# A recommendation tower's interaction layer: tiles of 16 rows by 8 columns of d in place of 4 by 32, and one sum over d for each group of four tiles

## The reference

```python
x0 = inputs; prev = inputs; outs = []
for W in filters:                                  # [1024, 128], then [32*128, 128]
    z = jnp.einsum('bhd,bmd->bhmd', x0, prev)      # products of two fields at the same d
    b, h, m, d = z.shape
    z = z.reshape(b, h * m, d)
    cur = jax.nn.relu(jnp.einsum('bpd,pn->bnd', z, W[0]))
    prev = cur
    outs.append(cur)
return jnp.sum(jnp.concatenate(outs, axis=1), axis=-1)   # the sum over d
...
h = jnp.concatenate([z, dense_ctx], axis=1)
h = jnp.maximum(h @ W_top1 + b_top1, 0.0)
h = jnp.maximum(h @ W_top2 + b_top2, 0.0)
y = h @ W_top3
```

## Time and profile before

| | us |
|---|---|
| median of 3 runs | 900.58 (899.3 to 905.62) |
| the profiled execution | 904.71 |
| its span, first to last instruction | 902.9 |
| PE busy | 879.3 (97%) |
| ACT busy | 782.9 (87%) |
| DVE busy | 780.5 (86%) |
| POOL busy | 750.6 (83%) |

### The profile page before, as it was taken

One profiled execution on the slowest core, in us unless ns is written; L12 is line 12 of the kernel. 1 busy time (PEld: TensorE's weight loads), 2 busy tenths in 40 slices (PEclk: granted clock), 3 DMA queues, 4 the chain that ended last, 5 costly groups with the idle time before them and its releaser, 6 DMA issues.

```text
span 902.9 us, 17442 instructions
## 1 busy us (share of the span) xinstructions
PE 879.3 (97%) x3758; PEld 689.7 (76%) x3758; DVE 780.5 (86%) x903; ACT 782.9 (87%) x2744; POOL 750.6 (83%) x542
## 2 busy tenths in 40 slices
PE   3899999999999999999999999999999999999988
PEld 2678877777887777788777778877777887777844
DVE  4588888999888899988889998888989888898991
ACT  2699899999989999999989999989999999999942
POOL 5599889898888989888898988889899898988430
PEclk9999999999999999999999999999999999999987
DMA  5432222221222222122222212222221122220000
GB/s 179 127 115 79 80 74 78 78 64 34 67 78 73 77 78 68 33 64 78 73 77 78 68 35 61 78 73 77 78 75 33 56 78 73 77 78 1 1 1 0
DMA packets 42810, 60.85 MB, mean 67 GB/s; under 512 B 6274, under 2 KB 17154, under 8 KB 42787
## 3 DMA queue, kind: packets, MB, share of 16 engines
q1 hardware_dynamic: 38690, 58.48, 21.1%
q0 software_dynamic: 4096, 2.11, 1.6%
HBM read 56.37 MB, written 4.20 MB: 67 GB/s over the span
## 4 chain that ended last, share of the span: by engine, by line
PE 95%; DMA 1%; ACT 1%; DVE 1%; issue 1%; POOL 0%; SPq 0%; DVEq 0%; ACTq 0%; POOLq 0%
PE ps_y L637 27%; PE ps_y L643 26%; PE ps_y L638 26%; PE ps_c L616 6%; PE ps_h L648 2%; PE ps_c L625 2%; PE ps_c L624 2%; PE ps_c L626 2%; PE ps_c L622 1%; ACT prod L399 1%; PE ps_y L694 1%; PE ps_y L693 1%; DMA second<-et_scratch 1%; DMA gat<-table,rows_now 0%; POOL gat L292 0%
## 5 line engine op out<-in xcount | busy, mean ns | idle before, releaser
L399 ACT ACTIVATE prod<-ps_y,es 128x128 f32<-128x128 f32 x2560 | 715.7, 434 | 72.7 <-PE ps_y L643 68.7
L537 DVE TENSOR_REDUCE csum<-prod 128x64 f32<-128x1536 f32 x256 | 447.3, 1748 | 10.4
L637 PE MATMUL ps_y<-w_hi,c_hi 128*128 128x512 f32 x1024 | 437.3, 427 | 2.1 <-ACT prod L399 1.3
L643 PE MATMUL ps_y<-w_hi,c_lo 128*128 128x512 f32 x1024 | 400.9, 392 | 0.0
L638 PE MATMUL ps_y<-w_lo,c_hi 128*128 128x512 f32 x1024 | 400.4, 391 | 0.0
L330 POOL TENSOR_TENSOR prod<-prod 128x1024 f32<-128x1024 f32 x128 | 308.3, 2408 | 55.6 <-ACT prod L399 48.8
L523 DVE TENSOR_TENSOR prod<-ps_y,es 128x512 f32<-128x512 f32 x384 | 256.8, 682 | 76.2 <-PE ps_y L643 72.8
L637 PEld LDWEIGHTS ps_y<-w_hi,c_hi 128*128 128x128 f32 x1024 | 192.8, 188 | 54.7 <-issue 18.2
L638 PEld LDWEIGHTS ps_y<-w_lo,c_hi 128*128 128x128 f32 x1024 | 192.9, 188 | 50.2 <-issue 14.9
L643 PEld LDWEIGHTS ps_y<-w_hi,c_lo 128*128 128x128 f32 x1024 | 192.1, 188 | 43.4
L321 POOL TENSOR_TENSOR z<-first,second 128x512 f32<-128x512 f32 x155 | 198.6, 1299 | 9.1 <-DMA second<-et_scratch 9.1
(11 more groups left out here) (65 smaller groups left out, 278.0 us busy)
## 6 DMA issues: line engine op xcount, KB each, us to landing
second<-et_scratch SPq DMA_DIRECT2D x160, 256.0 KB, 4.4
first<-et_scratch SPq DMA_DIRECT2D x32, 256.0 KB, 3.3
et_scratch<-gat SPq DMA_DIRECT2D x64, 64.0 KB
prod<-w SPq DMA_DIRECT2D x4, 512.0 KB, 7.1
gat<-table,rows_now POOLq DMA_INDIRECT x128, 2.4
wt_sb<-wt SPq DMA_DIRECT2D x2, 512.0 KB
prod<-w0a SPq DMA_DIRECT2D x1, 320.0 KB, 3.0
prod<-w0b SPq DMA_DIRECT2D x1, 320.0 KB, 3.3
```

The source lines that it names most:

```text
L399: last = nc.scalar.activation(prod[:, buffer_of(g, u), h // 2, :, h % 2], ps_y[:, bank_of(g, u, k), j * N:(j + 1) * N], ACT.Copy, scale=es ...
L537: nc.vector.tensor_reduce(csum[:, maps, 0], prod[:, buffer_of(g, u), FOLD // 2:F // 2, maps, :].rearrange("p a n t -> p n a t"), AX.XY, AL ...
L637: nc.tensor.matmul(out, hi, w_hi, start=True, stop=False)
L643: nc.tensor.matmul(out, lo, w_hi, start=False, stop=True).then_inc(y_ready, 1)
```

## The change

A tile is now all 16 rows of its group by 8 of the 32 d: tile o holds d from 8o to 8o + 7. Nothing is summed over d until all four tiles of a group are there: their rectified results are added element by element, and one matmul against a `ones_b` of 128 x 16 sums the rest. In pieces:

- The rows of a group are dealt to the gathers in another order (`ids`, made before launch), `turn` reads `gat` in runs of 8 elements, the layer-0 matmuls read z in runs of 8 in place of 32, and `sum_h0` reads `c` in runs of 8. Number and size of instructions stay.
- `reduce` writes `csum[:, g.r, maps, u]`, a column for each tile.
- `rectify` (DVE, 128 times) and the zeroed column go. `rectify_parts` (ACT, once a group, at (1, 6) of the next group) rectifies all four columns, 512 elements; `add_parts` (DVE, once a group, at (2, 4)) adds them to 128.
- `sum_h1` runs once a group at (3, 3), with 16 columns.
- After the loop ACT runs `rectify_parts` of the last group, then DVE `add_parts`, and PE one `sum_h1`.
- `ones_b` comes by one more transfer on SP's queue (8 KB), ahead of the loads of w1, in place of the memsets.

```diff
-        csum = sb("csum", [P, N, 2])
-        c1 = sb("c1", [P, 2, N])
-        ones_b = sb("ones_b", [P, BT])
+        csum = sb("csum", [P, SLOTS, N, TG])
+        c1_parts = sb("c1_parts", [P, N, TG])
+        c1 = sb("c1", [P, SLOTS, N])
+        ones_b = sb("ones_b", [P, GB])
...
+            sp.dma_start(ones_b[:, :], ones_of_b).then_inc(ones_in, 16)
...
+            def rectify_parts(g):
+
+                act.wait_ge(reduced, g.times(TG * HALVES, TG * HALVES))
+                wait(act, c1_ready, g.times(1))
+                nc.scalar.activation(c1_parts[:, :, :], csum[:, g.r, :, :], ACT.Relu).then_inc(parts_rectified, 1)
+
...
+                        if (u, k) == (1, 6) and number != 0:
+                            rectify_parts(g.plus(-1))
...
+            rectify_parts(LAST)
+            for groups in (range(GROUPS - 1), range(GROUPS - 1, GROUPS)):
+                act.wait_ge(h1_done, groups.stop)
...
-                nc.vector.transpose(es[:, g.r, :, :].rearrange("p u f -> p (u f)"), gat[:, g.r, :]).then_inc(es_ready, 1)
+                nc.vector.transpose(es[:, g.r, :, :], gat[:, g.r, :].rearrange("p (u o d) -> p o u d", u=TG, d=DT)).then_inc(es_ready, 1)
...
-                    h0[:, bass.ds(g.times(TG * BT), TG * BT)], c[:, :].rearrange("p (t d) -> p t d", d=D),
-                    AX.X, ALU.add).then_inc(h0_done, 1)
+                    h0[:, bass.ds(g.times(GB), GB)], c[:, :].rearrange("p (o b d) -> p b o d", b=GB, d=DT),
+                    AX.XY, ALU.add).then_inc(h0_done, 1)
...
-            def rectify(g, u):
-
-                dve.wait_ge(reduced, g.times(TG * HALVES, (u + 1) * HALVES))
-                wait(dve, h1_done, g.times(TG, u - 1))
-                nc.vector.tensor_reduce(c1[:, u % 2, :], csum[:, :, :], AX.X, ALU.max).then_inc(c1_ready, 1)
+            def add_parts(g):
+
+                dve.wait_ge(parts_rectified, g.times(1, 1))
+                nc.vector.tensor_reduce(c1[:, g.r, :], c1_parts[:, :, :], AX.X, ALU.add).then_inc(c1_ready, 1)
...
-                    nc.tensor.matmul(ps_c[:, :], w0_sum[:, k, :], z[:, k, :].rearrange("p (b u d) -> p u b d", u=TG, b=BT),
+                    nc.tensor.matmul(ps_c[:, :], w0_sum[:, k, :], z[:, k, :].rearrange("p (b o d) -> p o b d", b=GB, d=DT),
                                      start=(k == 0), stop=False)
...
-            def sum_h1(g, u):
-
-                pe.wait_ge(c1_ready, g.times(TG, u + 1))
-                nc.tensor.matmul(ps_h1[:, bass.ds(g.times(TG * BT, u * BT), BT)], c1[:, u % 2, :], ones_b[:, :],
+            def sum_h1(g):
+
+                pe.wait_ge(c1_ready, g.times(1, 1))
+                nc.tensor.matmul(ps_h1[:, bass.ds(g.times(GB), GB)], c1[:, g.r, :], ones_b[:, :],
                                  start=True, stop=True).then_inc(h1_done, 1)
...
-                        if k == 3 and not (number == 0 and u < 3):
-                            sum_h1(*before(g, u, 3))
+                        if (u, k) == (3, 3) and number != 0:
+                            sum_h1(g.plus(-1))
```

More of the change, by code:

```diff
@@ L34 @@
 BT = P // D
+GB = 16
+DT = P // GB
 TILES = B // BT
@@ L103, with tower @@
 LAST = Group((GROUPS - 1) // SLOTS, (GROUPS - 1) % SLOTS)
-def tower(nc, ids, bounds, copy_of, table, dense_t, w0a, w0b, w1, wt1, bt1, wt2, bt2, wt3, y):
+def tower(nc, ids, bounds, copy_of, ones_of_b, table, dense_t, w0a, w0b, w1, wt1, bt1, wt2, bt2, wt3, y):
     ctx = ExitStack()
@@ L176, in tower @@
         w0_step = sem("w0_step")
-        ones_zeroed = sem("ones_zeroed")
-        csum_zeroed = sem("csum_zeroed")
+        ones_in = sem("ones_in")
         rows_staged = sem("rows_staged")
@@ L201, in tower @@
         reduced = sem("reduced")
+        parts_rectified = sem("parts_rectified")
         c1_ready = sem("c1_ready")
@@ L433, in _ @@
             over_groups(act, body)
-            for tiles in (range(TILES - 2), range(TILES - 2, TILES)):
-                act.wait_ge(h1_done, tiles.stop)
-                cols = slice(BT * tiles.start, BT * tiles.stop)
+            rectify_parts(LAST)
+            for groups in (range(GROUPS - 1), range(GROUPS - 1, GROUPS)):
+                act.wait_ge(h1_done, groups.stop)
+                cols = slice(GB * groups.start, GB * groups.stop)
                 nc.scalar.activation(h1_hi[:, cols], ps_h1[:, cols], ACT.Copy).then_inc(h1_hi_ready, 1)
@@ L463, in _ @@
             nc.vector.tensor_scalar(rows[:, :], neg[:, :], bounds_sb[:, 2:3], None, ALU.add).then_inc(rows_step, 1)
[L465 to L470, removed]
             dve.wait_ge(w0_in, 48)
@@ L534, in reduce @@
                     dve.wait_ge(dve_scaled, signals(DVE_BANKS, g, u, NK - 1))
-                    wait(dve, c1_ready, g.times(TG, u))
                 maps = slice(half * N // HALVES, (half + 1) * N // HALVES)
-                nc.vector.tensor_reduce(csum[:, maps, 0], prod[:, buffer_of(g, u), FOLD // 2:F // 2, maps, :].rearrange("p a n t -> p n a t"),
+                nc.vector.tensor_reduce(csum[:, g.r, maps, u], prod[:, buffer_of(g, u), FOLD // 2:F // 2, maps, :].rearrange("p a n t -> p n a t"),
                                         AX.XY, ALU.add).then_inc(reduced, 1)
-            def rectify(g, u):
-                dve.wait_ge(reduced, g.times(TG * HALVES, (u + 1) * HALVES))
-                wait(dve, h1_done, g.times(TG, u - 1))
-                nc.vector.tensor_reduce(c1[:, u % 2, :], csum[:, :, :], AX.X, ALU.max).then_inc(c1_ready, 1)
+            def add_parts(g):
+                dve.wait_ge(parts_rectified, g.times(1, 1))
+                nc.vector.tensor_reduce(c1[:, g.r, :], c1_parts[:, :, :], AX.X, ALU.add).then_inc(c1_ready, 1)
             for k in range(NK):
@@ L579, in body @@
                             reduce(*before(g, u, 2), 1)
-                        if k == 4 and not (number == 0 and u < 2):
-                            rectify(*before(g, u, 2))
+                        if (u, k) == (2, 4) and number != 0:
+                            add_parts(g.plus(-1))
                         if k == 6 and not (number == 0 and u == 0):
@@ L596, in _ @@
             reduce(LAST, TG - 2, 1)
-            rectify(LAST, TG - 2)
             for half in range(HALVES):
                 reduce(LAST, TG - 1, half)
-            rectify(LAST, TG - 1)
+            add_parts(LAST)
             dve.wait_ge(h1_hi_ready, 2)
@@ L619, in layer0 @@
                 pe.wait_ge(z_lo_ready, g.times(SPLIT, k + 1 - WHOLE))
-                high, low = (x[:, k, :].rearrange("p (b u d) -> p u b d", u=TG, b=BT) for x in (z_hi, z_lo))
+                high, low = (x[:, k, :].rearrange("p (b o d) -> p o b d", b=GB, d=DT) for x in (z_hi, z_lo))
                 if k == LASTK:
@@ L677, in body @@
                             layer0(g.plus(1), z_used_at.index((u, k)))
-                        if k == 3 and not (number == 0 and u < 3):
-                            sum_h1(*before(g, u, 3))
+                        if (u, k) == (3, 3) and number != 0:
+                            sum_h1(g.plus(-1))
             over_groups(pe, body)
-            sum_h1(LAST, TG - 3)
             pe.wait_ge(top_in, 7 * 16)
@@ L695, in _ @@
             pe.wait_ge(h1_hi_ready, 1)
-            sum_h1(LAST, TG - 2)
-            sum_h1(LAST, TG - 1)
+            sum_h1(LAST)
             pe.wait_ge(top_lo_ready, 2)
@@ L767 @@
     arrays = {
-        "ids": np.ascontiguousarray(x["ids"].reshape(TILES, BT, F).transpose(1, 2, 0).reshape(P, TILES)),
+        "ids": np.ascontiguousarray(x["ids"].reshape(GROUPS, BT, TG, F).transpose(1, 3, 0, 2).reshape(P, TILES)),
         "bounds": np.tile(np.stack([counts - 1, counts, bases], 1).astype(np.float32), (BT, 1)),
         "copy_of": np.tile(np.array([[0, 0], [1, 0], [0, -1], [0, 0]], np.float32), (F, 1)),
+        "ones_of_b": np.kron(np.eye(GB, dtype=np.float32), np.ones((DT, 1), np.float32)),
         "table": np.concatenate(tables),
```

2 lines of the change are left out of this document (1 added, 1 removed).

## The result

| | before | after |
|---|---|---|
| median of 4 runs each, us | 899.94 (898.35 to 905.62) | 873.47 (872.53 to 874.27) |
| the profiled execution, us | 904.71 | 874.27 |
| its span, us | 902.9 | 872.5 |
| mean granted clock over the span, of 2.4 GHz | 0.989 | 0.996 |

The ratio of the times is 0.969, with a 95% interval of 0.966 to 0.973: 26.5 us faster, where 877 with a range of 871 to 889 was forecast. Seven more runs of the changed kernel in a later comparison gave 873.87 beside 898.09.

A forecast was written before the change was run, and what follows sets the result against it. PE's own instruction sequence was taken to bound the loop, DVE holding PE up in the last group. Terms of -20.9 + 0.6 - 2.6 - 0.5 = -23.4 us took the median 900.6 to 877, range 871 to 889.

The forecast's parts named there:

- Term 1: PE's sums over d: 91 fewer at 0.23 us, -20.9 us; 16 columns in the 30 that stay, +0.6 us.
- Term 2: Layer-0 matmuls on PE reading z in runs of 8: taken as 0, up to +9.1 us, a gain excluded.
- Two thirds to all of the excess: Layer-0 matmuls: this share of their 0.013 us over plain ones is there without breaks, as in the top network.
- Term 3: New ACTIVATE on ACT behind bank (1, 6): at most 0.8 us a group, hidden from PE, cost 0.
- 0.6 are left: ACT's waits of 2.1 us a group, less 0.8 new work and 0.7 shorter group, leave 0.6 us.
- Rival 4: ACT's new work delays PE's ring in each group: 19 to 25 us come back, 896 to 902; chance 0.08.
- Term 4: Work leaving DVE: worth nothing in the loop; in the last group L693 starts 2.6 us earlier.
- Term 5: The end: 16 fp32 instructions keep 14.0 us at the low clock; the last two sums become one, -0.5 us.
- other case: At the end the clock stays at 2.4 GHz: fp32 instructions take 7 us, PE waits for DVE, 4.6 us sooner.
- The start: Before the loop: the memsets lie beside transfers, one more 8 KB transfer goes ahead of w1's; cost 0.

The follow-up runs named there:

- The experiment: The changed kernel with the last group's two casts of the top weights moved from DVE to ACT: 870.85 us, ratio 0.966 to the kernel before.

## Why the prediction was right

**Term 1** held: 0.233 us a sum by experiment, 0.23 in the prediction; 30 groups x 0.700 = 21.0 us. The 16 columns, put at +0.6, cost nothing that a start shows (0.915 us for the three steps with a sum before and after; the trace before held no sum of 16, so that only the profile after bears this out). The Trainium skill's floor of about 25 ns (TensorE: Matmul & The Clock Gate, section Back-to-back issue gap), taken as the whole cost, would by estimate have made three sums 0.15 us; the chip took 0.70. The two instructions of a sum do start 0.026 us apart; the cost stands behind them, 0.112 to the next plain matmul and another 0.085 to the one after. That exposed weight loads are the reason, as the prediction says, was not tested.

**Term 2** was put at 0, with a gain ruled out, and there was one. "A gain is excluded: nothing is read in longer runs than before" took for granted that longer runs can't be worse. Runs of 8 gave 0.087 us a group against runs of 32 128 elements apart, 30 x 0.087 = 2.6 us. Start by start, the kernel with three sums put back differs from the kernel before only from chunk 2's first matmul on. The two triples, each with the three plain matmuls behind it, are 0.026 and 0.025 us shorter. Much of the rest is in layer-1 matmuls further behind: the nine that follow chunk 2's start 0.227 us apart on average where it had been 0.229 (0.021 us in all), and the stretch up to chunk 4 gives another 0.017. In the kernel before with chunk 2 read in runs of 8, chunk 2 and what follows up to chunk 3 got shorter by the same 0.047 us. So how layer 0 reads z is the cause, and it also works on the matmuls behind, most of which lie outside the table's six steps. ("Two thirds to all of the excess" for contiguous operands was misread, too: 0.70 between 0.68 and 0.72 is half by the earlier trace rows.) The table's rows follow neither the length of the runs nor their distance in a simple way, and why they differ by some nanoseconds stays open. With terms 1 and 2 the loop's 23.6 us are accounted for.

**Term 3** came to the right conclusion by wrong numbers. ACT got 0.52 us a group, not 0.8, since its records overlap; and it had at least 3.0 us of room, not the 2.1 of its waits. "0.6 are left" was at least 1.7. Rival 4 was therefore further off than its 0.08: between two and six more such instructions, not at the first.

**Term 4** foresaw 2.6 us in the last group and got 1.7. The missing 0.9 is, as far as 0.8 of it goes, the cast that became longer beside the fold. The prediction had taken durations in the last group as fixed. PE's ring waits at (2, 2) for DVE's bank (1, 4), which stands directly behind this cast: the bank ends at 835.40 and PE goes on at 835.55, after a wait of 1.17 us (858.56, 858.71 and 0.69 before). The experiment shows that DVE paces this stretch; that the 0.8 comes from the place of the fold rests on the two pairs of timelines and on the DVE rectifier, where moving it was tried.

**Term 5** took the low clock as before. The profile shows its "other case", and its price: 4.6 us said, 4.7 measured, with the wait for DVE's result that it named. In the runs at large both happen, so which case a profile shows is luck. The gain at equal mean clock is about 25 us (medians 898.3 to 873.8 at 0.996, 897.7 to 872.7 at 0.998); the other 1.5 us of the 26.5 go with executions that kept more of their clock.

**The start**, put at nothing, cost 0.5 us in the profiled pair. Its first layer-1 matmul varies between 29.3 and 31.7 us over the profiles, so this is no finding.

The sum, -23.4 us, was thus nearly the gain at equal clock (-25), with 2.6 of gain missed in term 2, 0.6 in term 1's columns, and 0.9 too much in term 4, which offset each other in part. The mechanism that carries it, fewer sums on PE, was right: 21.0 us.

## What to carry to other kernels

The cost of a small matmul in a stream of long ones is read from the starts around it, with and without it, and not from its columns or its record; here 0.233 us for 4 or 16 columns alike, so fewer sums pay and, between these two, narrower ones don't. Before work is moved to an engine with room, price it by starts rather than by records and waits, and look at what runs on the other engines at that very place: the same rectifier on DVE cost 0.40 us at one step and 2.3 at another, which was all of the gain.

## What the hardware showed unexpectedly

- A DVE `tensor_scalar` of 512 fp32 elements, SBUF to SBUF, started during a POOL `tensor_tensor`, ended only 0.29 us behind it: 2.34 us for 0.40. DVE's casts of the top weights did the same, 0.28 to 0.55 us behind. DVE's `tensor_reduce` was not held: one of 512 elements started at 421.16, during a POOL `tensor_tensor` (420.77 to 422.28), and took 0.69, and in the changed kernel the 79 `reduce` that began during a fold took 1.74 us, like the 126 with none beside them.
- A moving operand read in single fp32 elements 16 bytes apart runs at half rate (0.45 us for 0.23); runs of four and more do not.
- ACT's records of 512 elements from SBUF last 0.63 to 0.93 us in the rows shown and start 0.52 apart.
- Executions of one program differ by up to 9 us (895.8 to 904.6), in step with the mean granted clock; in two profiles of the kernel before, the clock was 1.2 GHz for one stretch of 17 us at the end.
- A different order of reading in one matmul also moves the start distances of the plain matmuls behind it by some nanoseconds (from 0.229 to 0.227 us over nine of them).
